# A decoder block on one core: second routing weight from its minimum, second choice, A's second values and three weight splits moved

## The chip, the cores and the metric

One Trainium2 chip, one core. The metric is the device time of one execution in microseconds; less is better. The core has TensorE (PE), VectorE (DVE), ScalarE (ACT), GpSimd (POOL) and SyncE (SP), each with its own in-order stream of instructions. Semaphores order them against each other, and they are written out by hand in this kernel.

## What is computed

`x` is 128 sequences of 64 tokens of width 128 in float32; `ctx` has the same shape.

```python
x = x + attn(layernorm(x))           # A: causal linear attention, 16 heads of 8, rope, elu + 1
x = x + xattn(layernorm(x), ctx)     # B: softmax attention over ctx, no projections, scale 8 ** -0.5
x = x + ffn(layernorm(x))            # C: shared expert + the best 2 of 8 experts

# inside ffn, xf = its input:
xn = norm(xf) * ln_scale + ln_bias
probs = softmax(xn @ gate_w.T)                     # 8 experts
tk_probs, tk_idx = top_k(probs, 2)
tk_probs = tk_probs / (sum(tk_probs) + 1e-5)
out = swiglu(xf, sWg, sWu, sWd)                    # hidden width 256
out += w[:, e] * swiglu(xf, Wg[e], Wu[e], Wd[e])   # for each e of the two chosen
```

## The kernel before

The 8192 tokens are 64 tiles of 128 and 16 groups of four tiles. The kernel has three stages.

**Steps.** A software pipeline of unrolled steps, s = -3 to 15, handles six groups at once: in step s, A's scores and values are those of group s (called a), A's projection that of f = s + 1, A's output and B's context that of h = s - 1, B's scores, softmax and values those of b = s - 2, c = s - 3 is normalised for C, and d = s - 4 is routed. Routing works on batches of two groups, so it has work only where d is odd, thus in odd steps from s = 5 on (`batch_of`, `batch_number`). Each engine has its own `step` function, and its lines are that engine's order: TensorE's at L832, ScalarE's at L1181, GpSimd's at L1494, VectorE's at L1918. In each step, scores come in four parts j = 0 to 3 (`scores`, L639), for A into `pair_x`, for B into `pair_y`; ScalarE cuts A's (`a_mask`, L1097), VectorE takes B's row maximum and subtracts it (`b_shift`, L1714 and L1718), ScalarE takes the exponential (L1126), TensorE transposes it (`b_probs_T`, L727), ScalarE copies it out (L1132), and 64 small matmuls of `a_values` (L671) or `b_values` (L744) make the values. `a_divide` (L1682, L1686) and `b_divide` (L1725 to L1733) divide by the sums on VectorE. `a_rope` (L1437) on GpSimd and `a_rotate` (L1656) on VectorE rotate queries and keys; TensorE turns and adds them (`a_q_T`, `a_k_T`, L572 and L573); `a_exp` (L1082, L1085) on ScalarE and `a_feature` (L1676) on VectorE make elu + 1. GpSimd builds the block-diagonal operands `Qblk` and `Kblk` (L1413). `c_statistics`, GpSimd's roots (L1356 to L1405), `c_norm` (L1044), `c_norm_T` (L759), its copy (L1146) and `c_logits` (L770) bring a group of C to its logits.

**Routing of a batch.** VectorE's `c_softmax` subtracts the smallest negated logit (`c_q`, zero for the best expert); ScalarE takes exp(-c_q) (`c_exp`, L1157). `c_first` marks the first choice, `c_second` finds the second minimum (L1784) and marks the second choice (L1788, L1789, `c_sel`). TensorE counts positions from `c_sel` (`c_positions`, L781 and L784), `c_index` makes indices, and `c_weights` the two weights: it multiplies both marks with the exponentials (L1800), sums the two and the whole (L1803), and divides (L1805 to L1808). It stands between the third `b_shift` and `a_divide(a, 0)`. GpSimd then scatters each token's row to its two experts' lists in DRAM (`c_scatter`, L1465), eight scatters per group, spread over the next step and a half. The last two batches are routed in the drain.

**Drain with the shared expert.** From 509 us on TensorE works the shared expert group by group (`s_up` L814, `s_down` L828, about 4.5 us per group), and the loop over 16 groups on VectorE (`drain`, L1989) and ScalarE (L1272) carries the last batches of routing and the tables between. GpSimd's drain (L1542) has the rest of the scatters and, between them, the low parts of the eight experts' weights (`split_weights`, L1482), each behind its high part from ScalarE (L1179). SyncE writes eight padding blocks once 12 groups are through `s_down` (L451, L471), then waits for all scatters (L477) and loads the first tiles (L458). TensorE transposes the first two tiles (L965) ahead of the last `s_down`.

**Routed tiles.** 135 tiles of 128 rows go through their expert (L965, L987, L997, L1009), are scaled (L1310) and scattered back by GpSimd (L1619); VectorE adds them.

Of the kernel before, what the change touches and what calls it, by code (L numbers as in the profile page):

```python
# [114 lines left out]
PAD_BEHIND = 12  # L115
E_RING = 6
TILE_BITS = 7
C_STEPS = 18
X_FIRST = 4 * GT
ROW_SLOTS = 4  # L120
B_LOADS = 4
SET_ZERO, SET_DVE = 9, 7
Y_RING = 4
# [48 lines left out]
def decoder_block(nc, x, ctx, mask, wq, wk, wv, wo, ln_scale, ln_bias, gate_w, wg, wu, wd, swg, swu, swd,  # L172
# [5 lines left out]
    with ExitStack() as stack:  # L178
# [130 lines left out]
        def tile_entry(kind, n):  # L309
# [30 lines left out]
            b_e b_eT_ps b_eTd b_av b_rc b_qt b_yd  # L340
            c_st c_ag c_xf c_cp c_var c_xfT_ps c_xfTd c_lg_ps c_lgd c_ch c_ex c_seld
# [3 lines left out]
            f_xT_ps f_xTd f_xTl w_hi w_lo f_up f_si f_hd f_hT_ps f_hTd f_dn f_yd  # L345
            y_ad y_sum y_st""".split()
# [155 lines left out]
        def _(pe):  # L502
# [329 lines left out]
            def step(s, par):  # L832
# [32 lines left out]
                scores(a, b, 2, par)  # L865
                if on(a):
                    a_values(a, 1, par)
                if on(d) and batch_of(d):
# [5 lines left out]
                if on(c):  # L874
                    c_norm_T(c, h, odd)
                if on(b):
                    b_probs_T(b, 1, a, 2)
# [92 lines left out]
            pe.wait_ge(S["ffw_in"], (2 + CH) * 16)  # L970
            pe.wait_ge(S["w_lo"], 1 + E)

# [59 lines left out]
        def _(act):  # L1032
# [111 lines left out]
            def c_norm_evac(c, par):  # L1144
                act.wait_ge(S["c_xfT_ps"], c + 1)
                act.copy(xfT[:, c * GN:(c + 1) * GN], banks[FRONT1][:, :]).then_inc(S["c_xfTd"], 1)  # L1146

            def c_second_row(c, par):

                act.wait_ge(S["c_xf"], GT * c + GT)  # L1150
                act.copy(c_row[:, c % ROW_SLOTS, :, 1, 0:D], c_row[:, c % ROW_SLOTS, :, 0, 0:D]).then_inc(S["c_cp"], 1)
# [29 lines left out]
            def step(s, par):  # L1181
# [38 lines left out]
                if on(f):  # L1220
                    a_exp(f)
                if on(b):
                    b_exp(b, 2)
# [103 lines left out]
        def _(pool):  # L1327
# [214 lines left out]
            def drain():  # L1542
# [44 lines left out]
                for n in range(GT):  # L1587
                    send(before_last, TOP * n, TOP * n + TOP)
                    if n < GT - 1:
                        split_weights(3 + n)  # L1590
                for n in range(GT):
                    send(last, TOP * n, TOP * n + TOP)
                    if n < 2:
                        split_weights(6 + n)

# [37 lines left out]
        def _(dve):  # L1633
# [139 lines left out]
            def c_first(d):  # L1773
                n, chain = c_chain(d)
                q, hit, pick = c_q[:, 0:n, :], c_hit[:, 0, 0:n, :], c_pick[:, 0, 0:n, :]
                chain(dve.scalar_tensor_tensor(hit, q, 0.0, per_expert(order, n), ALU.is_equal, ALU.mult), 4)
                chain(dve.tensor_reduce(c_m[:, 0:n], hit, AX, ALU.max), 5)
                chain(dve.tensor_tensor(pick, per_expert(order, n), per_token(c_m[:, :], n), ALU.is_equal), 6)
                chain(dve.scalar_tensor_tensor(c_t[:, 0:n, :], pick, TAKEN, q, ALU.mult, ALU.add), 7)

            def c_second(d):
                n, chain = c_chain(d)
                t, hit, pick = c_t[:, 0:n, :], c_hit[:, 0, 0:n, :], c_pick[:, 1, 0:n, :]
                chain(dve.tensor_reduce(c_min[:, 1, 0:n], t, AX, ALU.min), 8)  # L1784
                chain(dve.tensor_tensor(hit, t, per_token(c_min[:, 1, :], n), ALU.is_equal), 9)
                chain(dve.tensor_tensor(hit, hit, per_expert(order, n), ALU.mult), 10)
                chain(dve.tensor_reduce(c_m[:, 0:n], hit, AX, ALU.max), 11)
                chain(dve.tensor_tensor(pick, per_expert(order, n), per_token(c_m[:, :], n), ALU.is_equal), 12)  # L1788
                dve.tensor_tensor(c_sel[:, 0:n, :], c_pick[:, 0, 0:n, :], pick, ALU.add).then_inc(S["c_seld"], 1)  # L1789

            def slots_of(d):
                slot, n = batch_of(d)[0] % ROW_SLOTS, len(batch_of(d))
                return slice(slot, slot + n)

            def c_weights(d):

                n, chain = c_chain(d)
                dve.wait_ge(S["c_ex"], batch_number(d) + 1)
                dve.wait_ge(S["c_idxd"], batch_number(d) + 1)
                chain(dve.tensor_tensor(c_hit[:, 0:TOP, 0:n, :], c_pick[:, :, 0:n, :],  # L1800
                                        c_e[:, 0:n, :].rearrange("p (o t) e -> p o t e", o=1).to_broadcast([P, TOP, n, E]),
                                        ALU.mult), 13)
                chain(dve.tensor_reduce(c_best[:, :, 0:n], c_hit[:, :, 0:n, :], AX, ALU.add), 14)  # L1803
                m = c_m[:, 0:n]
                chain(dve.scalar_tensor_tensor(m, c_best[:, TOP, 0:n], TOP_EPS, c_best[:, 0, 0:n], ALU.mult, ALU.add), 15)  # L1805
                chain(dve.tensor_tensor(m, m, c_best[:, 1, 0:n], ALU.add), 16)
                chain(dve.reciprocal(m, m), 17)
                chain(dve.tensor_tensor(c_row[:, slots_of(d), :, :, D].rearrange("p s t n -> p n (s t)"), c_best[:, 0:TOP, 0:n],  # L1808
                                        m.rearrange("p (o t) -> p o t", o=1).to_broadcast([P, TOP, n]), ALU.mult),
                      C_STEPS)  # L1810

# [95 lines left out]
            def s_hidden(i, c):  # L1907
                dve.wait_ge(S["s_si"], i * CH + c + 1)
                dve.tensor_tensor(s_h[:, i % 2, c, :], s_sg[:, c, :], banks[S_UP[c][1]][:, :], ALU.mult)\
                    .then_inc(S["s_hd"], 1)  # L1910

            def s_add(i):
                dve.wait_ge(S["s_dn"], i + 1)
# [4 lines left out]
            def step(s, par):  # L1918
# [14 lines left out]
                if on(c):  # L1933
                    c_statistics(c)
                if on(b):
                    b_shift(b, 1)
# [26 lines left out]
            def drain():  # L1963
# [23 lines left out]
                c_first(last - 2)  # L1987
                c_second(last - 2)
                for i in range(GROUPS):  # L1989
                    s_hidden(i, 0)  # L1990
                    if i == 0:
                        b_divide(last, 1)
                    if i == 1:
                        c_weights(last - 2)
                    if i == 2:
# [3 lines left out]
                    if i == 6:  # L1999
                        c_first(last)  # L2000
                    if i == 8:
                        c_weights(last)
                    s_hidden(i, 1)
# [8 lines left out]
                    if i == 6:  # L2012
                        c_second(last)
                    if i == 7:
                        c_index(last)
# [8 lines left out]
                    if i == 12:  # L2024
                        tile_table()
                    if i:
                        s_add(i - 1)
# [10 lines left out]
            dve.wait_ge(S["set_d"], 4)  # L2038
            one_of_two = query[:, :].rearrange("p (m c) -> p c m", c=C)
# [80 lines left out]
```

## Time and profile before

| | us |
|---|---|
| median of 3 runs | 815.31 |
| lowest and highest of them | 813.89, 822.11 |
| the profiled execution's own time | 821.73 |
| its span | 819.9 |
| busy: TensorE 737.6, VectorE 596.5, ScalarE 572.3, GpSimd 553.7 | |
| mean granted clock of TensorE | 0.967 |

The span goes from the first to the last instruction of the profiled execution; times in rows count from its start. Idle time of an engine that isn't on the chain costs nothing. In a row, what stands in brackets is the idle time of the engine ahead of it and what ended it; "issue" means that the profile shows nothing that it waited for.

### The profile page before, as it was taken

What the parts mean: (1) busy time and instruction counts of PE and PEld (TensorE: products, weight loads), DVE (VectorE), ACT (ScalarE), POOL (GpSimd) and SP (SyncE); (2) the same over time, 40 slices, a digit from 0 to 9 for tenths busy, and PEclk for the clock granted to TensorE, in tenths of its full rate; (3) what the DMA queues carried; (4) which work ended last, traced back from release to release, by engine and by line L of the source; (5) the groups of instructions that cost most, each with busy time, mean ns of one, the idle gap of its engine ahead of it and who ended that gap; (6) DMA issues with size and microseconds to landing.
All of it is one profiled execution on the core that took longest, in us unless ns stands there. A gap on an engine that the chain in (4) does not pass through costs nothing.

```text
span 819.9 us, 36399 instructions
## 1 busy us (share of the span) xinstructions
PE 737.6 (90%) x14413; PEld 588.2 (72%) x14413; DVE 596.5 (73%) x1484; ACT 572.3 (70%) x1117; POOL 553.7 (68%) x706
## 2 busy tenths in 40 slices
PE   8889989988988898898898787999899999999993
PEld 4556677767766666676676565888789999987882
DVE  2335867878988987988978697669467777787773
ACT  4577879889889788988877584464256666665661
POOL 6575447469889788888877775587536666665563
PEclk9998989999999999999999898899989999999997
DMA  8421022022202203211220205010233333476673
GB/s 222 107 55 53 4 55 55 19 56 69 73 27 72 71 23 75 68 52 49 68 71 30 68 22 168 29 40 25 69 76 92 92 91 91 118 213 195 180 207 115
DMA packets 78147, 66.91 MB, mean 82 GB/s; under 512 B 8975, under 2 KB 68248, under 8 KB 77984
## 3 DMA queue, kind: packets, MB, share of 16 engines
q1 hardware_dynamic: 68512, 47.14, 22.3%
q0 software_dynamic: 8416, 16.93, 6.3%
q8 instruction: 120, 1.97, 1.0%
q10 hardware_dynamic: 1056, 0.52, 0.2%
q14 instruction: 43, 0.35, 0.2%
HBM read 42.46 MB, written 22.56 MB: 79 GB/s over the span
## 4 chain that ended last, share of the span: by engine, by line
PE 38%; issue 20%; POOL 15%; ACT 12%; DVE 10%; SPq 3%; DMA 2%; POOLq 0%; DVEq 0%; ACTq 0%
POOL mixed L1619 7%; PE pair_x L727 5%; PE pair_x L635 5%; ACT Am L1097 4%; PE bank L744 3%; POOL routed L1465 3%; PE pair_x L987 3%; PE bank L671 3%; PE bank L552 3%; ACT ExT L1132 2%; DVE mx L1714 2%; PE bank L1009 2%; DVE Ex L1718 2%; PE pair_y L627 2%; PE pair_y L635 1%
## 5 line engine op out<-in xcount | busy, mean ns | idle before, releaser
L1619 POOL DMA_INDIRECT mixed<-f_y,f_x x135 | 131.0, 971 | 91.2 <-issue 64.7
L1465 POOL DMA_INDIRECT routed<-c_row,c_idx x128 | 130.7, 1021 | 50.3 <-issue 32.9
L1305 ACT ACTIVATE qk<-pair_x 128x256 f32<-128x256 f32 x135 | 51.9, 384 | 60.8 <-PE pair_x L987 60.8
L1009 PEld LDWEIGHTS bank<-Qblk,Am 128*128 128x128 f32 x540 | 79.9, 191 | 18.9 <-issue 8.0
L1009 PE MATMUL bank<-Qblk,Am 128*128 x540 | 83.8, 278 | 2.5 <-DVE Am L2062 1.2
L1413 POOL TENSOR_TENSOR Qblk<-qT,con 128x512 f32<-128x512 f32 x64 | 66.4, 1046 | 28.4 <-DVE qT L1676 28.0
L1714 DVE TENSOR_REDUCE mx<-pair_y 128x16 f32<-128x1024 f32 x64 | 77.3, 1208 | 9.4 <-PE pair_y L635 9.4
L1097 ACT ACTIVATE Am<-pair_x 128x1024 f32<-128x1024 f32 x64 | 65.0, 1015 | 25.3 <-PE pair_x L635 25.3
L1718 DVE TENSOR_TENSOR Ex<-pair_y,mx 128x1024 f32<-128x1024 f32 x64 | 78.4, 1224 | 2.2
L1132 ACT COPY ExT<-pair_x 128x1024 f32<-128x1024 f32 x64 | 64.5, 1008 | 21.0 <-PE pair_x L727 19.4
L727 PE MATMUL pair_x<-con,Ex 128*128 128x128 f32 x512 | 68.9, 278 | 9.8 <-ACT Am L1097 9.8
L635 PE MATMUL pair_y<-Kblk,KQ 32*64 32x256 f32 x1024 | 74.3, 402 | 1.3 <-issue 1.3
L2057 DVE TENSOR_TENSOR rot<-qk,pair_x 128x256 f32<-128x256 f32 x135 | 56.8, 421 | 24.8 <-ACT qk L1305 24.5
L635 PE MATMUL pair_x<-Qblk,KQ 32*64 32x256 f32 x1024 | 73.1, 399 | 0.0
L1126 ACT ACTIVATE Ex<-Ex 128x1024 f32<-128x1024 f32 x64 | 67.3, 1052 | 3.6 <-DVE Ex L1718 3.5
L727 PEld LDWEIGHTS pair_x<-con,Ex 128*128 128x128 f32 x512 | 56.1, 141 | 16.8 <-issue 13.4
L1437 POOL TENSOR_TENSOR phi<-qk,con 128x512 f32<-128x512 f32 x32 | 35.7, 1134 | 47.6 <-ACT qk L1064 47.6
L1413 POOL TENSOR_TENSOR Kblk<-ctxT,con 128x512 f32<-128x512 f32 x64 | 66.9, 1059 | 1.0 <-PE pair_y L635 0.3
L987 PE MATMUL pair_x<-wup_hi,f_xT_hi 128*128 x135 | 65.7, 487 | 0.0
L744 PE MATMUL bank<-Cblk,ExT 128*32 128x18 f32 x4096 | 51.0, 188 | 14.5 <-issue 11.4
L744 PEld LDWEIGHTS bank<-Cblk,ExT 128*32 128x32 f32 x4096 | 43.8, 111 | 27.3 <-issue 20.5
L671 PEld LDWEIGHTS bank<-Vblk,Am 128*32 128x32 f32 x4096 | 43.4, 112 | 24.3 <-issue 21.1
(222 smaller groups left out, 1974.9 us busy)
## 6 DMA issues: line engine op xcount, KB each, us to landing
f_x<-routed SPq DMA_DIRECT2D x135, 65.0 KB, 1.9
ctxD<-in_ctx SPq DMA_DIRECT2D x32, 256.0 KB
ctxP<-in_ctx SPq DMA_DIRECT2D x16, 256.0 KB
maskB<-in_mask_BxS_if SPq DMA_DIRECT2D x16, 256.0 KB
Cblk<-mixed SPq DMA_DIRECT2D x8, 512.0 KB
Kblk<-mixed SPq DMA_DIRECT2D x8, 512.0 KB, 4.0
block_out<-X SPq DMA_DIRECT2D x14, 256.0 KB
mixed<-f_y,f_x POOLq DMA_INDIRECT x135, 2.6
```

Of the source, the lines that this page charges most:

```text
L635: return pe.matmul(banks[first_bank + q // C][half * T:(half + 1) * T, s * RH * T:(s + 1) * RH * T], stationary[rows, par, (2 * j + s) * T ...
L727: ins = pe.transpose(banks[s][:, rp * P:(rp + 1) * P], Ex[:, j % 2, rp // 2, s, rp % 2 * 2:rp % 2 * 2 + 2, :] .rearrange("p r n -> p (r n) ...
L744: ins = pe.matmul(banks[B_O][s * T + q:s * T + q + TQ, at:at + 2 * E9], ExT[:, j % 2, s, 2 * i + r, 1 - c, q:q + TQ], Cblk[:, par, 2 * j + ...
L987: ins = pe.matmul(banks[F_UP[n % 2]][:, :], x_part[:, u % 3, :], w_part[:, bass.ds(e, 1), :, :].rearrange("p o m i -> p (o m i)"), start=( ...
L1009: ins = pe.matmul(banks[F_O[n % 2]][:, 0:D], f_hT[:, u % 3, c * P:(c + 1) * P], wdn[:, bass.ds(e, 1), c, :].rearrange("p o d -> p (o d)"), ...
L1097: act.activation(Am[:, j % 2].rearrange("p i s r n -> p (i s r n)"), pair_x[:, :], ACT.Relu)\
L1132: act.copy(ExT[:, j % 2].rearrange("p s r c q -> p (s r c q)"), pair_x[:, :]).then_inc(S["b_eTd"], 1)
L1413: return pool.tensor_tensor(dst[:, j, :, :, :], both.to_broadcast([P, 2, RH, T]), rows, ALU.mult)
L1465: pool.indirect_dma_start(routed[:, :], bass.IndirectOffsetOnAxis(ap=c_idx[:, d % ROW_SLOTS, t, n:n + 1], axis=0), c_row[:, d % ROW_SLOTS, ...
L1619: pool.indirect_dma_start(mixed[:, :], bass.IndirectOffsetOnAxis(ap=f_x[:, u, D + 1:D + 2].bitcast(I32), axis=0), f_y[:, u, :], None, boun ...
L1714: dve.tensor_reduce(mx[:, j % 2, :], scores, AX, ALU.max).then_inc(S["b_mx"], 1)
L1718: dve.tensor_tensor(Ex[:, j % 2].rearrange("p i s r n -> p (i s r) n"), scores, mx[:, j % 2, :].rearrange("p (r o) -> p r o", o=1).to_broa ...
```

## The change

1. `c_weights`: the best expert's exponential is 1, and the second's is exp(-second minimum). `c_best[:, 0]` is set to 1 once; in the steps `c_best[:, 1]` comes from a new instruction on ScalarE, `c_exp_second`, which stands behind `a_exp`; VectorE sums the eight exponentials and goes on from there, with a wait for the new semaphore `c_e2` behind that sum. For the two batches of the drain VectorE makes it from the mark and the exponentials (`c_second_picked`). The chain of a batch has 17 links instead of 18.
2. `c_second` is cut: the mark of the second choice and `c_sel` become `c_chosen`, which in a step stands behind `b_divide(c, 1)` and `c_statistics(c)`. `c_first` waits for the indices of the batch before.
3. TensorE: `a_values(a, 1)` moves from ahead of `c_positions` to behind `a_k_T` and `c_norm_T`.
4. The low parts of experts 5 to 7 are made by VectorE in groups 13 to 15 of the drain. GpSimd keeps five, and sends the last group's scatters in one go. TensorE waits for both counts before the first tile.

```diff
+BY_POOL = 5
-C_STEPS = 18
+C_STEPS = 17
-SET_ZERO, SET_DVE = 9, 7
+SET_ZERO, SET_DVE = 9, 8
...
@@ TensorE, step
                 scores(a, b, 2, par)
-                if on(a):
-                    a_values(a, 1, par)
                 if on(d) and batch_of(d):
                     c_positions(d, h)
                 if on(b):
...
                 if on(c):
                     c_norm_T(c, h, odd)
+                if on(a):
+                    a_values(a, 1, par)
                 if on(b):
                     b_probs_T(b, 1, a, 2)
...
-            pe.wait_ge(S["w_lo"], 1 + E)
+            pe.wait_ge(S["w_lo"], 1 + BY_POOL)
+            pe.wait_ge(S["w_ld"], E - BY_POOL)
@@ ScalarE
+            def c_exp_second(d):
+
+                n = len(batch_of(d)) * GT
+                act.wait_ge(S["c_ch"], C_STEPS * batch_number(d) + 8)
+                act.activation(c_best[:, 1, 0:n], c_min[:, 1, 0:n], ACT.Exp, scale=-1.0).then_inc(S["c_e2"], 1)
...
                 if on(f):
                     a_exp(f)
+                if on(d) and batch_of(d):
+                    c_exp_second(d)
                 if on(b):
                     b_exp(b, 2)
@@ GpSimd, drain
-                    if n < GT - 1:
+                    if n < BY_POOL - 3:
                         split_weights(3 + n)
-                for n in range(GT):
-                    send(last, TOP * n, TOP * n + TOP)
-                    if n < 2:
-                        split_weights(6 + n)
+                send(last, 0, TOP * GT)
@@ VectorE
             def c_first(d):
                 n, chain = c_chain(d)
+                if batch_number(d):
+                    dve.wait_ge(S["c_idxd"], batch_number(d))
...
                 chain(dve.tensor_reduce(c_m[:, 0:n], hit, AX, ALU.max), 11)
+
+            def c_chosen(d):
+                n, chain = c_chain(d)
+                pick = c_pick[:, 1, 0:n, :]
                 chain(dve.tensor_tensor(pick, per_expert(order, n), per_token(c_m[:, :], n), ALU.is_equal), 12)
                 dve.tensor_tensor(c_sel[:, 0:n, :], c_pick[:, 0, 0:n, :], pick, ALU.add).then_inc(S["c_seld"], 1)
...
+            def c_second_picked(d):
+
+                n, picked = len(batch_of(d)) * GT, batch_number(d) - (BATCHES - 2) + 1
+                dve.wait_ge(S["c_ex"], batch_number(d) + 1)
+                dve.wait_ge(S["c_idxd"], batch_number(d) + 1)
+                dve.tensor_tensor(c_hit[:, 0, 0:n, :], c_pick[:, 1, 0:n, :], c_e[:, 0:n, :], ALU.mult).then_inc(S["c_pe"], 1)
+                dve.wait_ge(S["c_pe"], picked)
+                dve.tensor_reduce(c_best[:, 1, 0:n], c_hit[:, 0, 0:n, :], AX, ALU.add).then_inc(S["c_e2"], 1)
+
             def c_weights(d):
 
                 n, chain = c_chain(d)
                 dve.wait_ge(S["c_ex"], batch_number(d) + 1)
-                dve.wait_ge(S["c_idxd"], batch_number(d) + 1)
-                chain(dve.tensor_tensor(c_hit[:, 0:TOP, 0:n, :], c_pick[:, :, 0:n, :],
-                                        c_e[:, 0:n, :].rearrange("p (o t) e -> p o t e", o=1).to_broadcast([P, TOP, n, E]),
-                                        ALU.mult), 13)
-                chain(dve.tensor_reduce(c_best[:, :, 0:n], c_hit[:, :, 0:n, :], AX, ALU.add), 14)
-                m = c_m[:, 0:n]
-                chain(dve.scalar_tensor_tensor(m, c_best[:, TOP, 0:n], TOP_EPS, c_best[:, 0, 0:n], ALU.mult, ALU.add), 15)
-                chain(dve.tensor_tensor(m, m, c_best[:, 1, 0:n], ALU.add), 16)
-                chain(dve.reciprocal(m, m), 17)
+                m, e_sum, e_best = c_m[:, 0:n], c_best[:, TOP, 0:n], c_best[:, 0:TOP, 0:n]
+                chain(dve.tensor_reduce(e_sum, c_e[:, 0:n, :], AX, ALU.add), 13)
+                dve.wait_ge(S["c_e2"], batch_number(d) + 1)
+                chain(dve.tensor_scalar(m, e_sum, TOP_EPS, 1.0, ALU.mult, ALU.add), 14)
+                chain(dve.tensor_tensor(m, m, c_best[:, 1, 0:n], ALU.add), 15)
+                chain(dve.reciprocal(m, m), 16)
...
+            def split_weights(e):
+
+                dve.wait_ge(S["w_hi"], e + 2)
+                dve.tensor_tensor(wup_lo[:, e, :, :], wup[:, e], wup_hi[:, e, :, :], ALU.subtract).then_inc(S["w_ld"], 1)
...
                 if on(c):
                     c_statistics(c)
+                if on(d) and batch_of(d):
+                    c_chosen(d)
                 if on(b):
                     b_shift(b, 1)
@@ VectorE, drain: c_chosen directly behind each c_second, c_second_picked ahead of each c_weights, and
+                    if i >= GROUPS - (E - BY_POOL):
+                        split_weights(E - (GROUPS - i))
                     if i:
                         s_add(i - 1)
@@ set-up
+            dve.memset(c_best[:, 0, :], 1.0).then_inc(S["set_d"], 1)
```

## Rows read from the trace of the kernel before

**Rows 1.** The page: shares of the chain by engine; then one group, GpSimd's tile scatters

```profile
PE 38%; issue 20%; POOL 15%; ACT 12%; DVE 10%; SPq 3%; DMA 2%; POOLq 0%; DVEq 0%; ACTq 0%
...
L1619 POOL DMA_INDIRECT mixed<-f_y,f_x x135 | 131.0, 971 | 91.2 <-issue 64.7
```

**Rows 2.** Chain that ended last, around the end of the drain: start, us, what

```profile
586.45 2.42 DMA routed<-c_row,c_idx
```

**Rows 3.** GpSimd's timeline near the end of the drain: start us, us, what

```profile
570.05 1.71 POOL L1482 TENSOR_TENSOR wup_lo<-KQ,wup_hi 128x512 fp32r<-128x512 f32 x1 [0.57 <-ACT wup_hi L1179]
571.93 0.99 POOL L1465 DMA_INDIRECT routed<-c_row,c_idx  x1 [0.16 <-issue]
573.22 0.97 POOL L1465 DMA_INDIRECT routed<-c_row,c_idx  x1 [0.30 <-issue]
...
576.86 1.32 POOL L1482 TENSOR_TENSOR wup_lo<-KQ,wup_hi 128x512 fp32r<-128x512 f32 x1
```

**Rows 4.** Timelines of SyncE's queue and of TensorE, 574 to 598

```profile
576.62 8.56 SPq L451 DMA_DIRECT2D routed<-pad  x8
589.69 2.56 SPq L458 DMA_DIRECT2D f_x<-routed  x3
...
587.20 1.95 PE L828 MATMUL bank<-shared_down_w,Vblk 128*128 128x128 f32 x16
591.65 0.41 PE L965 MATMUL pair_y<-con,f_x 128*128 128x128 f32 x1 [2.51 <-DMA f_x<-routed]
...
593.00 3.62 PE L828 MATMUL bank<-shared_down_w,Vblk 128*128 128x128 f32 x16
```

**Rows 5.** Windows: stretch, length, busy us of each engine (count), PEclk, DMA share, GB/s

```profile
167.00:171.00 4.00, 3.85 (x110) 2.70 (x108) 3.03 (x11) 3.68 (x6) 2.22 (x5) 1.00 0.05 16
459.50:463.00 3.50, 2.78 (x84) 1.67 (x92) 1.31 (x4) 1.62 (x2) 3.25 (x10) 0.50 0.06 19
593.00:595.00 2.00, 2.00 (x11) 2.00 (x11) 0.29 (x1) 0.27 (x1) 0.00 (x0) 0.50 0.24 60
```

**Rows 6.** TensorE's timeline: first and last of five gaps behind A's second values

```profile
165.17 0.24 PE L744 MATMUL bank<-Cblk,ExT 128*32 128x18 f32 x2 [1.25 <-issue]
...
457.25 0.24 PE L744 MATMUL bank<-Cblk,ExT 128*32 128x18 f32 x4 [2.69 <-issue]
```

**Rows 7.** L1800 and L1157 by source (ns min/median/max); VectorE's timeline at 586

```profile
L1800 DVE TENSOR_TENSOR c_hit<-c_pick,c_hit x8: 281/1140/2691, 166.6 to 554.2; 128x128 f32<-128x128 f32 x8
...
L1157 ACT ACTIVATE c_hit<-c_q x8: 238/246/258, 148.2 to 547.3; 128x64 f32<-128x64 f32 x8
...
586.67 0.69 DVE L1909 TENSOR_TENSOR Vblk<-phi,pair_y 128x512 f32<-128x512 f32 x1 [1.32 <-ACT phi L1173]
```

**Rows 8.** Timelines of VectorE, ScalarE, TensorE, 399 to 412; ScalarE, TensorE, 170 to 177

```profile
400.09 2.56 DVE L1800 TENSOR_TENSOR c_hit<-c_pick,c_hit 128x128 f32<-128x128 f32 x1
...
403.07 0.17 DVE L1805 SCALAR_TENSOR_TENSOR c_m<-c_best 128x8 f32<-128x8 f32 x1
...
405.90 0.68 DVE L1676 SCALAR_TENSOR_TENSOR qT<-bank,qk 128x512 f32<-128x512 f32 x1
...
408.35 1.22 DVE L1718 TENSOR_TENSOR Ex<-pair_y,mx 128x1024 f32<-128x1024 f32 x1
...
405.04 1.04 ACT L1126 ACTIVATE Ex<-Ex 128x1024 f32<-128x1024 f32 x1
...
411.03 0.39 PE L627 MATMUL pair_y<-bias,couple 64*128 64x512 bf16 x2 [0.40 <-issue]
...
170.81 1.04 ACT L1126 ACTIVATE Ex<-Ex 128x1024 f32<-128x1024 f32 x1
...
176.90 0.39 PE L627 MATMUL pair_y<-bias,couple 64*128 64x512 bf16 x2 [0.40 <-issue]
```

**Rows 9.** Timelines of VectorE and TensorE, 386 to 394

```profile
386.82 1.06 DVE L1788 TENSOR_TENSOR c_pick<-con,c_m 128x64 f32<-128x64 f32 x1
...
393.90 0.39 PE L627 MATMUL pair_y<-bias,couple 64*128 64x512 bf16 x2 [0.82 <-DVE Ex L1718]
```

More of the change, by code:

```diff
@@ L340, in decoder_block @@
             b_e b_eT_ps b_eTd b_av b_rc b_qt b_yd
[L341 removed]
+            c_st c_ag c_xf c_cp c_var c_xfT_ps c_xfTd c_lg_ps c_lgd c_ch c_ex c_e2 c_pe c_seld
             c_ps c_posd c_read c_idxd c_put c_next c_tick c_sc0 c_sc1 c_sc2 c_sc3
@@ L344, in decoder_block @@
             s_xh s_xl s_up s_si s_hd s_dn s_ac
-            f_xT_ps f_xTd f_xTl w_hi w_lo f_up f_si f_hd f_hT_ps f_hTd f_dn f_yd
+            f_xT_ps f_xTd f_xTl w_hi w_lo w_ld f_up f_si f_hd f_hT_ps f_hTd f_dn f_yd
             y_ad y_sum y_st""".split()
@@ L1782, in c_second @@
                 n, chain = c_chain(d)
-                t, hit, pick = c_t[:, 0:n, :], c_hit[:, 0, 0:n, :], c_pick[:, 1, 0:n, :]
+                t, hit = c_t[:, 0:n, :], c_hit[:, 0, 0:n, :]
                 chain(dve.tensor_reduce(c_min[:, 1, 0:n], t, AX, ALU.min), 8)
@@ L1798, in c_weights @@
                 dve.wait_ge(S["c_ex"], batch_number(d) + 1)
-                dve.wait_ge(S["c_idxd"], batch_number(d) + 1)
-                chain(dve.tensor_tensor(c_hit[:, 0:TOP, 0:n, :], c_pick[:, :, 0:n, :],
-                                        c_e[:, 0:n, :].rearrange("p (o t) e -> p o t e", o=1).to_broadcast([P, TOP, n, E]),
-                                        ALU.mult), 13)
-                chain(dve.tensor_reduce(c_best[:, :, 0:n], c_hit[:, :, 0:n, :], AX, ALU.add), 14)
-                m = c_m[:, 0:n]
-                chain(dve.scalar_tensor_tensor(m, c_best[:, TOP, 0:n], TOP_EPS, c_best[:, 0, 0:n], ALU.mult, ALU.add), 15)
-                chain(dve.tensor_tensor(m, m, c_best[:, 1, 0:n], ALU.add), 16)
-                chain(dve.reciprocal(m, m), 17)
-                chain(dve.tensor_tensor(c_row[:, slots_of(d), :, :, D].rearrange("p s t n -> p n (s t)"), c_best[:, 0:TOP, 0:n],
+                m, e_sum, e_best = c_m[:, 0:n], c_best[:, TOP, 0:n], c_best[:, 0:TOP, 0:n]
[4 more added lines that the diff above has]
+                chain(dve.reciprocal(m, m), 16)
+                chain(dve.tensor_tensor(c_row[:, slots_of(d), :, :, D].rearrange("p s t n -> p n (s t)"), e_best,
                                         m.rearrange("p (o t) -> p o t", o=1).to_broadcast([P, TOP, n]), ALU.mult),
@@ L1988, in drain @@
                 c_second(last - 2)
+                c_chosen(last - 2)
                 for i in range(GROUPS):
@@ L1993, in drain @@
                     if i == 1:
+                        c_second_picked(last - 2)
                         c_weights(last - 2)
@@ L2001, in drain @@
                     if i == 8:
+                        c_second_picked(last)
                         c_weights(last)
@@ L2013, in drain @@
                         c_second(last)
+                        c_chosen(last)
                     if i == 7:
@@ L2037, in _ @@
             dve.tensor_tensor(query[:, :], ident[:, 0:T], ident[:, T:2 * T], ALU.add).then_inc(S["set_d"], 1)
-            dve.wait_ge(S["set_d"], 4)
+            dve.wait_ge(S["set_d"], 5)
             one_of_two = query[:, :].rearrange("p (m c) -> p c m", c=C)
```

## Prediction

> **What bounds the kernel now.** I read the chain of work that ended last first, then the timelines of the engines that it names, then granted clock by window. The chain has no single owner: TensorE 38%, "issue" 20%, GpSimd 15%, ScalarE 12%, VectorE 10% [rows 1]. So each edit has to be priced at its own place. There are three.
>
> The steps (about 29 us each, up to 499 us). In the middle of a step ScalarE runs without a gap and TensorE waits for it. In an odd step, where a batch of eight tiles is routed, VectorE carries more than in an even one.
>
> The drain (509 to 590 us). TensorE is full, but the chain that ends last is GpSimd's: one scatter after the other behind the last product of `c_weights` (L1808), the last one's landing from 586.45 on [rows 2], then SyncE's loads and the first tile.
>
> The routed tiles (from 590 us). GpSimd sends the 135 tiles off one after the other, 0.97 us each and half a microsecond of "issue" between (64.7 us for 126) [rows 1]: it paces the stage from the first one on. Nothing there is edited, so the stage moves as a block.
>
> **The change, part by part.** All sums are against the profiled execution: 821.73 us, span 819.90, so 1.83 lies around it. The median of the runs shown is 815.31; I take the same difference from it.
>
> *Three splits leave GpSimd.* The first one stands for 0.57 of waiting, 1.71 of work and 0.16 to the next scatter, 2.44 us, where two scatters in a row have 0.30 between them: 2.14 saved. The other two cost 1.32 and again some 0.17, 1.2 saved each [rows 3]. Together 4.5: the last scatter lands at 584.4 and not 588.9. But another chain is next. SyncE's eight padding writes start at 576.62 behind TensorE's twelfth group and are issued until 585.2 [rows 4]; of 65 KB each, like the tile loads, they should land 1.9 later, near 587.1. So the first load moves from 589.69 by about 1.8, not by 4.5. TensorE is free at 589.15 (587.20 + 1.95) and now waits 2.51 for the first tile; that shrinks to some 0.75, with a second pause of 0.8 for the second tile, whose load is issued 1.1 later (three loads in 2.56) [rows 4]. That brings a second gain. Behind the pause of now the last `s_down` took 3.62 us against 1.95, at clock 0.50 [rows 4, 5], and the first two tiles some 0.5 more. A pause of 1.25 left the clock at 1.00, one of 2.69 took it to 0.50 [rows 5, 6]. The two pauses together, 1.55, lie nearer to the first. I take 1.8 + 1.7 + 0.5 = 4.0 saved. Bounds: 1.8 (clock falls all the same) and 4.5.
>
> The trace shows a fall behind a long pause and none behind a shorter one. The Trainium skill (TensorE: Matmul & The Clock Gate, What's actually happening) says that the gate goes by how busy the array was lately, not by one pause, so two short ones with a 0.3 us transpose between them may act as one. By that rule the sum would keep 1.8 of the 4.0.
>
> VectorE takes the three splits in the last three groups. A product over the same 128x512 (L1909) takes 0.69, and VectorE waits 0.7 to 1.3 us for ScalarE ahead of each one there [rows 7]; a split delays one `s_add` whose bank is needed a group later. So: nothing. Without that cover it would be 2.1.
>
> *`c_weights`.* Before: the product L1800 (0.28 undisturbed), a sum over 192 elements, then four small ones of 0.2 to 0.25 each with their gaps (the first at 403.07) [rows 7, 8]; 1.6 in all. After, in a step: one sum over a third of the elements (some 0.2), then again four small ones. In the drain a product and a sum more stand ahead, some 0.25 each: 1.6, no change. In four of the steps L1800 takes 2.0 to 2.7 [rows 7, 8] because GpSimd builds two blocks just then. That is VectorE's time, yet it is no gain, by the next point.
>
> *The new wait.* `c_weights` now waits for an exponential on ScalarE that stands behind `a_exp`. VectorE comes to `c_weights` at 400.09; `a_exp` is over at 405.04, where L1126 follows it [rows 8]. Behind the wait on VectorE stand both divisions, `a_feature`, the fourth `b_shift`; the first scores of the next step need that. From there (call it E): the exponential 0.2 (over 8 elements; the one over 64 takes 0.25 [rows 7]); four small instructions and the two divisions 2.83 (403.07 to 405.90); feature and shift 3.67 (405.90 to the end of L1718, 409.57); start of TensorE 0.14. Sum: L627 at E + 6.84. In the five odd steps that have an `a_exp` it now stands at E + 6.09, 6.74, 5.94, 6.77, 5.99 (the first and the last shown) [rows 8]. So 0.75, 0.10, 0.90, 0.07, 0.85 later, 2.7 together. In the two small ones another path counts: A's third values wait for A's division (E + 1.9, where they start at E + 1.4 and 1.6), and ScalarE is 0.2 longer: 0.5 for both instead of 0.2. Sum 3.0 lost. Bounds: 0.2 per step for the exponential alone, 1.0; and the whole lateness of `a_feature` (E + 3.03 against 0.13, 2.33, 1.39, 1.95 and 0.86), 8.5.
>
> *Second choice behind the statistics.* In two steps the marking collides with GpSimd's rotation: L1788 and L1789 take 1.06 and 0.97 instead of 0.22, and L627 then waits 0.82 for VectorE [rows 9]. Behind the division and the statistics, 2.5 us later, the rotation is over, so two waits of 0.8 go: 1.6 gained. The positions are needed some 7 us on. That c's statistics, and GpSimd's root with them, come earlier I count at nothing: ScalarE is busy until it wants them. Bounds 0 and 3.0 (VectorE's whole loss).
>
> The row shows two VectorE instructions held by one on GpSimd. The Trainium skill (SBUF — State Buffer, Who interferes with whom) says that a VectorE instruction with two SBUF inputs contends with a GpSimd one that reads SBUF, and that `tensor_scalar` may contend too. By it, the marking would meet the small operations for c's root that the statistics have just released; at 0.2 each (six steps) the sum would lose 1.2.
>
> *A's second values behind the keys.* 64 matmuls, 0.7 us, go behind `c_norm_T`. The keys come 0.7 earlier but ScalarE is busy until the transposed tokens anyway, and `b_probs_T` starts 0.2 later inside the same cover. I take 0. Bounds: 0.2 in 16 steps, 3.2 lost; or, since two runs of 64 short matmuls no longer stand together, the five gaps of TensorE that lie there (1.25 the first, 2.69 the last, 7.8 in all) gone [rows 6].
>
> *The rest.* `c_first` waits for the indices of the batch before, which VectorE itself wrote in an earlier step: nothing. One memset more in the set-up lies beside the loads of the weights: nothing, and 0.1 without them.
>
> Net: 3.0 − 1.6 − 4.0 = −2.6 us: 819.1 for the profiled execution, 812.7 for the median.
>
> **The rivals.**
> *The gaps go.* TensorE's gaps "issue" come where short matmuls are dense: five in b's values, the keys or c's transposes right behind A's second values. Spread out, they vanish: −7.8 more, 804.9. Against it: three of the places that stay dense have gaps too, and behind a gap ScalarE is often late anyway. [...]
> *The wait for the exponential is passed on whole.* The place is VectorE at `c_weights`; it decides once the next step has no slack left for late queries and shift. Price 8.5 for 3.0: −2.6 + 5.5 = +2.9, 818.2, slower than before. For it: chain and ScalarE are tight there. Against it: VectorE idles 2 to 3 us early in the next step.
> *The clock falls again* at 591: 1.8 for 4.0, −0.4, 814.9.
> *The splits weren't the drain's bound*, because the pads land later than thought: drain 0 and the rest as forecast, +1.4, 816.7.
>
> **How the numbers follow.** Chances: forecast 0.45, gaps 0.15, exponential 0.15, clock 0.17, pads 0.08. Each but the first is one departure from the forecast; the range goes from the gaps' 805 to 820 (exponential and clock together, 820.4). A measurement tells about 1%, 8.2 us, from no change. Faster by that needs the gaps: 0.17. Slower by that needs 823.5, exponential, 3.2 for the moved values and no gain in the drain: 0.06. Within: 0.77.
>
> **What would show it.** Right: no L1482 after the fifth; last scatter near 582; first L965 near 590; `s_down` 1.95 at clock 1.00. An idle of 3 to 5 us on VectorE ahead of the second instruction of `c_weights`, released by ScalarE, five times; L627 of the next step released by VectorE's shift. L1788's line at 0.22 throughout. Wrong: last scatter early and first load not; odd steps longer by over 1 us each; TensorE's "issue" idle before 500 us well under 20 us.

## The result, and the profile after the change

The changed kernel takes 819.03 us (median of 20 runs, 816.01 to 829.01) against 814.30 (20 runs) for the kernel before: ratio 1.0051, 95% interval 1.003 to 1.0072, so 2.4 to 5.9 us slower. A second series of the same kernel, g1 below, gave 1.0072. The forecast was 2.6 us less. The profiled execution took 826.73 us, span 824.2; single executions of one kernel differ by up to 15 us, so a single profile shows where time goes better than how much.

The chain of work that ended last, by engine:

```profile
PE 38%; issue 18%; DVE 14%; ACT 12%; POOL 12%; SPq 3%; DMA 2%; POOLq 0%; DVEq 0%; ACTq 0%
```

VectorE had 10% of it and GpSimd 15% [rows 1]: the end is reached through VectorE more often. Where, its timeline in the step of [rows 8] tells:

```profile
401.26 0.21 DVE L1822 TENSOR_REDUCE c_best<-c_hit 128x8 f32<-128x64 f32 x1
406.95 0.17 DVE L1824 TENSOR_SCALAR c_m<-c_best 128x8 f32<-128x8 f32 x1 [5.48 <-ACT c_best L1154]
...
409.73 0.68 DVE L1683 SCALAR_TENSOR_TENSOR qT<-bank,qk 128x512 f32<-128x512 f32 x1
410.33 0.68 DVE L1683 SCALAR_TENSOR_TENSOR KQ<-bank,qk 128x512 f32<-128x512 f32 x1
```

ScalarE's timeline there, and TensorE's up to the next step's first scores, L628 (L627 in the kernel before):

```profile
405.69 1.06 ACT L1087 ACTIVATE qk<-qk 128x1024 f32<-128x1024 f32 x1
406.65 0.19 ACT L1154 ACTIVATE c_best<-c_min 128x8 f32<-128x8 f32 x1
406.75 1.04 ACT L1128 ACTIVATE Ex<-Ex 128x1024 f32<-128x1024 f32 x1
...
413.44 0.59 ACT L1122 COPY KQ<-bank 128x512 f32<-128x512 f32 x1 [1.72 <-PE bank L716]
```

```profile
411.06 1.06 PE L771 MATMUL bank<-gateT,xfT 128*128 128x8 f32 x8 [0.39 <-DVE KQ L1683]
412.05 0.77 PE L672 MATMUL bank<-Vblk,Am 128*32 128x18 f32 x64
412.75 0.66 PE L716 MATMUL bank<-con,b_xn 128*128 128x128 f32 x4
...
414.13 0.39 PE L628 MATMUL pair_y<-bias,couple 64*128 64x512 bf16 x2 [0.40 <-ACT KQ L1122]
```

The new wait is there: 5.48 us of idle VectorE, released by ScalarE's small exponential. Call E the start of the third exponential of B (L1126, now L1128), 406.75. `a_feature` starts at E + 2.98, as forecast (3.03). But L628 stands at E + 7.38 and not at E + 6.84. TensorE's logits (L771) wait for `a_feature`, whose bank they overwrite; behind them come 64 products of A's values, the four transposes of B's tokens, ScalarE's copy of them, and only then L628: 3.12 from the end of `a_feature` (411.01). In all five odd steps that have an `a_exp`, L771 starts 4.31 to 4.32 behind E, released by `a_feature`.

The drain, in the timelines of SyncE's queue, of GpSimd and of TensorE:

```profile
584.47 8.81 SPq L452 DMA_DIRECT2D routed<-pad  x8
596.90 9.10 SPq L459 DMA_DIRECT2D f_x<-routed  x9
```

```profile
589.89 0.97 POOL L1475 DMA_INDIRECT routed<-c_row,c_idx  x1 [0.30 <-issue]
```

```profile
595.06 1.95 PE L829 MATMUL bank<-shared_down_w,Vblk 128*128 128x128 f32 x16
598.79 0.33 PE L966 MATMUL pair_y<-con,f_x 128*128 128x128 f32 x1 [1.78 <-DMA f_x<-routed]
599.80 0.48 PE L966 MATMUL bank<-con,f_x 128*128 128x128 f32 x1 [0.68 <-DMA f_x<-routed]
600.07 3.41 PE L829 MATMUL bank<-shared_down_w,Vblk 128*128 128x128 f32 x16
```

The last scatter, seen from the steps' last L627 (499.05 before, 506.60 after), ends 4.1 us earlier (88.4, now 84.3); the first load of a tile moves by 0.3 only (90.6, now 90.3).
```profile
594.00:597.00 3.00, 3.00 (x22) 2.62 (x20) 1.80 (x3) 1.09 (x2) 0.00 (x0) 1.00 0.03 5
597.00:599.00 2.00, 0.22 (x2) 0.14 (x1) 0.77 (x2) 0.00 (x0) 0.00 (x0) 1.00 0.16 33
600.00:603.00 3.00, 3.00 (x15) 3.00 (x15) 0.29 (x1) 0.27 (x1) 0.00 (x0) 0.50 0.29 67
```

The marking of the second choice (its durations in ns: least, median, most) no longer collides, as forecast; in the kernel before it took 1.06 in [rows 9] and 1.09 at most:

```profile
L1801 DVE TENSOR_TENSOR c_pick<-con,c_m x8: 190/192/225, 155.9 to 556.4; 128x64 f32<-128x64 f32 x8
```

### The profile page after: what moved, and what is told of

It is laid out like the page before. It is cut to its first block, busy times and chain, and to the rows that moved or that the text cites. A ratio compares the mean times of both kernels' runs of the same rounds, so it can differ in the third digit from the quotient of the medians.

```text
span 824.2 us, 36412 instructions
## 1 busy us (share of the span) xinstructions
PE 736.9 (89%) x14413; PEld 584.8 (71%) x14413; DVE 582.6 (71%) x1484; ACT 571.4 (69%) x1123; POOL 549.1 (67%) x703
## 3 DMA queue, kind: packets, MB, share of 16 engines
q8 instruction: 119, 1.95, 1.1%
## 4 chain that ended last, share of the span: by engine, by line
PE 38%; issue 18%; DVE 14%; ACT 12%; POOL 12%; SPq 3%; DMA 2%; POOLq 0%; DVEq 0%; ACTq 0%
POOL mixed L1626 8%; PE pair_x L728 4%; PE pair_x L636 4%; ACT Am L1099 3%; PE bank L553 3%; PE bank L745 3%; PE pair_x L989 3%; PE bank L672 2%; DVE Ex L1725 2%; DVE mx L1721 2%; PE bank L1011 2%; PE bank L829 2%; ACT ExT L1134 2%; PE pair_y L815 2%; PE bank L771 2%
## 5 line engine op out<-in xcount | busy, mean ns | idle before, releaser
L1128 ACT ACTIVATE Ex<-Ex 128x1024 f32<-128x1024 f32 x64 | 67.3, 1051 | 3.4 <-DVE Ex L1725 3.2
L672 PE MATMUL bank<-Vblk,Am 128*32 128x18 f32 x4096 | 51.2, 188 | 17.7 <-ACT Am L1099 9.0
L1320 ACT ACTIVATE f_y<-bank,f_x 128x128 f32<-128x128 f32 x135 | 49.6, 368 | 15.6 <-PE bank L1011 8.1
```

What stands on the lines that cost most here:

```text
L672: ins = pe.matmul(num[s * T + q:s * T + q + TQ, r // RH, :, r % RH, :], Am[:, j % 2, r // RH, s, r % RH, q:q + TQ], Vblk[:, par, 2 * j + s ...
```

## The experiments

Three measures are read from every profile. *Ten periods*: from A's exponential (L1085 of the kernel before) in step 4 to the same in step 14, ten steps later. Five of them hold the place of the new wait (odd) and five hold the marking (even). *First result*: the first tile scatter (L1619 of before), counted from the steps' last L627. The ratio is to the kernel before, run on the same chip: e1 to e4 on one, f1 to f4 on a second, g1 to g4 on a third, h1 to h3 on a fourth. It rests on 6 runs of e4, f1, g3 and g4, 10 of h1, 12 of each of the others and 20 of the changed kernel; the other columns are of one profiled execution each.

| kernel | even | odd | ten periods | first result | ratio (95%) |
|---|---|---|---|---|---|
| before | 149.4 | 143.2 | 292.6 | 105.1 | |
| h2 before again | 147.1 | 143.5 | 290.7 | 103.3 | 1.0011 (0.9985-1.0037) |
| e2 splits only | 148.9 | 143.8 | 292.6 | 101.4 | 1.0019 (0.9996-1.0043) |
| e3 values only | 152.9 | 140.5 | 293.5 | 103.7 | 1.0025 (0.9991-1.0059) |
| f4 marking only | 146.5 | 143.1 | 289.6 | 103.2 | 0.9951 (0.9924-0.9978) |
| changed | 147.5 | 148.1 | 295.6 | 103.6 | 1.0051 (1.0030-1.0072) |
| g1 changed again | 147.5 | 148.9 | 296.3 | 102.6 | 1.0072 (1.0036-1.0108) |
| h1 splits back | 144.4 | 153.0 | 297.4 | 105.9 | 1.0079 (1.0046-1.0113) |
| e4 weights, splits | 147.9 | 148.9 | 296.8 | 101.2 | 1.0112 (1.0074-1.0151) |
| e1 early exponential | 144.8 | 141.8 | 286.6 | 103.1 | 0.9978 (0.9951-1.0006) |
| f2 e1, values back | 147.6 | 141.2 | 288.8 | 102.5 | 0.9936 (0.9906-0.9965) |
| f3 e1, marking back | 153.5 | 139.9 | 293.5 | 102.1 | 0.9968 (0.9934-1.0001) |
| g2 weights behind | 144.7 | 141.9 | 286.7 | 100.9 | 0.9955 (0.9929-0.9981) |
| f1 e1, early pads | 146.2 | 141.5 | 287.7 | 99.1 | 0.9880 (0.9846-0.9914) |
| h3 f1, splits back | 147.5 | 140.6 | 288.1 | 103.4 | 0.9946 (0.9915-0.9976) |
| g3 f1 with g2's move | 144.7 | 141.1 | 285.8 | 97.9 | 0.9896 (0.9862-0.9930) |
| g4 f1, values back | 143.8 | 142.7 | 286.5 | 97.9 | 0.9852 (0.9822-0.9883) |

**The wait.** Theory W: the wait for the exponential made the odd steps longer. Its rival, theory V: A's second values did.

e1 is the changed kernel with the small exponential earlier in ScalarE's `step`:

```
                     b_exp(b, 1)
+                if on(d) and batch_of(d):
+                    c_exp_second(d)
                 if on(c):
                     c_norm(c, odd)
...
                     a_exp(f)
-                if on(d) and batch_of(d):
-                    c_exp_second(d)
```

Expected of e1:

> The changed kernel with the exponential of the second weight moved up in ScalarE's order, to behind the second exponential of B, about 9 us ahead of the cut of A's exponential; all else as changed. Theory W (the wait): VectorE no longer waits some 5 us in c_weights, L628 of the next step stands 5.9 to 6.8 us behind the start of the third exponential of B instead of 7.4, the five odd steps get 5.5 us back in all, and the time is 5 us under the changed kernel, 0.998 of the kernel before (812 to 814). Theory V (A's second values behind the keys cost it): the wait goes but the time stays within 1.5 us of the changed kernel, 1.004 to 1.006 of before.

e3 moves one call in TensorE's `step` of the kernel before, as shown; e4 is the changed kernel with this call and `c_chosen(d)` back at their old places:

```
                 scores(a, b, 2, par)
-                if on(a):
-                    a_values(a, 1, par)
...
                     c_norm_T(c, h, odd)
+                if on(a):
+                    a_values(a, 1, par)
```

Expected of e3:

> The kernel before with A's second values behind the keys and c's transposes, and nothing else. Theory W: no cost of its own, 0.998 to 1.002 of before; the idle times of TensorE that nothing explains fall from 22.7 us to some 16 with no gain in time. Theory V: the cost of the change is here, 1.004 or more.

Expected of e4:

> The changed kernel with A's second values and the marking of the second choice back at their old places, so that only the new weights with their wait and the moved splits stay. Theory W: the wait costs 5.5 us in five odd steps, the splits give 1 to 2 back, the marking's collision with the rotation is back (two waits of 0.8 to 1 us): 3.5 to 5 us over before, 1.004 to 1.006. Theory V: at or under the time of before, 0.998 to 1.001.

g1 is the changed kernel unaltered; g2 moves one call on VectorE:

```
-                if on(d) and batch_of(d):
-                    c_weights(d)
                 if on(a):
                     a_divide(a, 0)
...
                     a_feature(f, odd)
+                if on(d) and batch_of(d):
+                    c_weights(d)
```

Expected of g1:

> The changed kernel, unaltered, on the same chip as the three that follow. 1.005 of before, 1.003 to 1.007, as first measured; L628 7.4 us behind the third exponential's start in five steps, ten periods 295 to 297 us.

Expected of g2:

> The changed kernel with c_weights behind a_feature on VectorE; the exponential stays where the change put it, behind a_exp. Theory F (the wait costs only because both divisions and a_feature stand behind it): a_feature starts at some 0.1 us behind the end of a_exp, L628 at 5.9 to 6.2 behind the third exponential's start, ten periods 286 to 288 us, 0.8 to 1 per cent under the changed kernel. Theory C (the odd steps are longer for ScalarE's extra instruction and TensorE's logits whatever VectorE does): L628 stays at 7 or more and the time within 2 us of the changed kernel.

The same step in e1, VectorE and TensorE (E is 394.69):

```profile
390.12 0.21 DVE L1822 TENSOR_REDUCE c_best<-c_hit 128x8 f32<-128x64 f32 x1
390.37 2.33 DVE L1824 TENSOR_SCALAR c_m<-c_best 128x8 f32<-128x8 f32 x1
...
395.32 0.68 DVE L1683 SCALAR_TENSOR_TENSOR qT<-bank,qk 128x512 f32<-128x512 f32 x1
```

```profile
400.63 0.39 PE L628 MATMUL pair_y<-bias,couple 64*128 64x512 bf16 x2 [0.40 <-ACT KQ L1122]
```

The five distances from E to the next L627 are 7.40, 7.38, 7.49, 7.38, 7.38 in the changed kernel and 7.39 to 7.76 in e4; in e1 they are 5.93, 7.07, 5.93, 6.70, 5.94, in g2 5.93 to 6.42. All four profiles with the wait ahead of the feature (the changed kernel, g1, h1, e4) have odd periods of 148 to 153 us, all others 139.9 to 143.8. V fell: e3 has no cost in the odd steps (140.5), and its 1.0025 has an interval that reaches 1.000. e4's odd periods bear W out, but its 1.0112 lies well over the expected 1.004 to 1.006. What made it 9 us slower its profile doesn't show; that execution was the fastest of e4's six, 816.87 against a median of 820.16. g2 keeps the exponential late and the wait stays harmless:

```profile
399.82 0.69 DVE L1683 SCALAR_TENSOR_TENSOR qT<-bank,qk 128x512 f32<-128x512 f32 x1
400.43 0.68 DVE L1683 SCALAR_TENSOR_TENSOR KQ<-bank,qk 128x512 f32<-128x512 f32 x1
401.03 0.21 DVE L1822 TENSOR_REDUCE c_best<-c_hit 128x8 f32<-128x64 f32 x1
401.27 0.17 DVE L1824 TENSOR_SCALAR c_m<-c_best 128x8 f32<-128x8 f32 x1
```

Theory F held: g2 is 1.2% under g1 by the ratios. So it isn't the wait that costs but what stands behind it on VectorE. That the path then runs through the logits is read from the rows; no run moved the logits.

**The marking.** f4 is the kernel before with the marking split off from `c_second` and placed as in the changed kernel; f3 is e1 with the marking back at its old place:

```
                     c_statistics(c)
+                if on(d) and batch_of(d):
+                    c_chosen(d)
```

Expected of f4:

> The kernel before with the marking of the second choice behind the division and the statistics, and nothing else. As forecast: both instructions at 0.22, two waits of 0.8 to 1.0 of L627 for VectorE gone, ten periods 290.6 to 291.2 instead of 292.6, time 0.998. If the marking and the early statistics are what the early exponential's kernel gains: 288 or less and 0.994.

Expected of f3:

> The changed kernel with the early exponential, and the marking of the second choice back right behind its comparison, ahead of the division and the statistics. If the marking collides with GpSimd's rotation as in the kernel before: L1788 and L1789 of before take about 1 us in two or more steps, the ten periods take 288 to 289 us, 1.6 to 2 more than with it moved; time 1.000. If the collision came from elsewhere: 286.6 and 0.998.

f4 lies between its two expectations: ten periods 289.6, ratio 0.9951. The forecast counted one wait of TensorE per collision. A collision in e3, on VectorE, GpSimd and TensorE, shows two:

```profile
266.69 1.06 DVE L1788 TENSOR_TENSOR c_pick<-con,c_m 128x64 f32<-128x64 f32 x1
267.79 0.96 DVE L1789 TENSOR_TENSOR c_sel<-c_pick 128x64 bf16<-128x64 f32 x1
```

```profile
266.64 2.03 POOL L1437 TENSOR_TENSOR phi<-qk,con 128x512 f32<-128x512 f32 x2 [0.82 <-ACT qk L1064]
```

```profile
273.78 0.39 PE L627 MATMUL pair_y<-bias,couple 64*128 64x512 bf16 x2 [0.82 <-DVE Ex L1718]
...
277.35 0.30 PE L572 MATMUL bank<-con,rot 128*128 128x128 f32 x1 [0.90 <-DVE c_hit L1825]
```

Against f4, VectorE stays 1.3 to 1.9 us late through the step, the keys (L572) wait too, for the bank that the positions hold, and the step up to ScalarE's next A exponential is 2.35 longer. The six profiles with the marking at its old place have even periods of 147.1 to 153.5, mean 150.0; the eleven with it moved 143.8 to 147.6, mean 145.9. f3's expectation missed in size (6 us and not 2) and in the ratio (0.9968 and not 1.000). In the two with the moved values and the old marking, e3 and f3, both instructions are slow together in four and in three steps, against two, one, two and two in the kernel before, h2, e2 and e4. So the price seems to hang on where the rotation falls against the marking; no run set that apart.

**The values.** f2 and g4 are e1 and f1 with the reverse of e3's edit.

Expected of f2:

> The changed kernel with the early exponential, and A's second values back ahead of B's first values. If the moved values are worth something once the wait is gone: the ten periods of the steps take 290 to 293 us instead of 286.6, and the time is 1.002 or more. If they are worth nothing, as forecast: 286 to 288 and the time of the early exponential, 0.998.

Expected of g4:

> The changed kernel with the early exponential and the early padding writes, and A's second values back at their old place. If the moved values are worth nothing: 0.988 like the kernel that has them moved. If the 1.6 us between ten-period sums of 287.2 and 288.8 are theirs: 0.990.

Neither expectation was met, and the two runs don't decide it. By the ten periods f2 is 1.6 us above the mean of e1 and f1 (287.2), g4 1.2 below f1; by the ratios both are the faster of their pair, by 0.4% and 0.3%, with intervals that meet and on different chips. Their worth stays open within 3 us.

**The drain.** Theory P (pads): SyncE's padding writes hold the first load of a tile once the scatters end earlier. Theory S: the scatters alone held it.

e2 is the kernel before with the change's `split_weights` on VectorE alone; g3 is f1 with g2's edit, and f1 is e1 with this:

```
-PAD_BEHIND = 12
+PAD_BEHIND = 11
```

Expected of e2:

> The kernel before with the three splits of weights moved to VectorE and nothing else. Theory P (pads: SyncE's padding writes land 3.6 us behind their last issue and hold the first load): the last scatter goes 4 us earlier, the first load of a tile only 0.5 to 0.9 us, and the time falls by 1 to 2 us, 0.998 of before. Theory S (GpSimd's scatters were the bound, as forecast): first load 1.8 us or more earlier, s_down in the pause at full clock, time 4 us lower, 0.995.

Expected of f1:

> The changed kernel with the early exponential, and SyncE's padding writes behind the eleventh group of the shared expert instead of the twelfth (PAD_BEHIND 11 for 12). Theory P (pads bind the first load): the writes go 4.5 us earlier, the first load of a tile follows the last scatter's landing and stands 86 to 87 us behind the last L627 of the steps instead of 89.5 to 90.3, TensorE no longer waits ahead of tile 0, s_down there takes 1.95 and the first scatter of a result comes at 99 to 100 instead of 101.3 to 103.7; time 2 to 3 us under the early exponential alone, 0.995 of before. Theory S (pads are not what the load waits for): load and time unchanged.

Expected of g3:

> The changed kernel with the early exponential, c_weights behind a_feature and the padding writes behind the eleventh group. If c_weights ahead of the divisions still costs something in the odd steps: one to two us under the pads-and-exponential kernel, 0.986 of before. If those steps are bound by ScalarE once the wait is gone: the same as it, 0.988.

SyncE's queue in f1, and TensorE there, with no wait and `s_down` at 1.95:

```profile
566.40 8.84 SPq L452 DMA_DIRECT2D routed<-pad  x8
579.88 5.20 SPq L459 DMA_DIRECT2D f_x<-routed  x5
```

```profile
581.96 1.95 PE L829 MATMUL bank<-shared_down_w,Vblk 128*128 128x128 f32 x16
583.74 0.27 PE L966 MATMUL pair_y<-con,f_x 128*128 128x128 f32 x1
583.85 0.27 PE L966 MATMUL bank<-con,f_x 128*128 128x128 f32 x1
583.96 1.95 PE L829 MATMUL bank<-shared_down_w,Vblk 128*128 128x128 f32 x16
```

P holds: the load at 86.3, the first result at 99.1. g3 and g4 repeat it (97.9). In time f1 gained more than expected (0.988 and not 0.995). g3's 0.9896, on another chip, is not under f1's 0.9880, so once the exponential is early, `c_weights` ahead of the divisions shows no further cost. In e2 the last scatter came 4 to 5 us earlier and the load 0.6 to 1.2, against h2 and the kernel before, as P says, but the ratio of 1.0019 shows nothing of the expected 1 to 2 us.

Three more runs were for the size of the drain's term and the rest of the loss. h1 and h3 are the changed kernel and f1 with the splits back on GpSimd, whose loop is then as before (VectorE's three calls and TensorE's second wait go with it):

```
-                    if n < BY_POOL - 3:
+                    if n < GT - 1:
                         split_weights(3 + n)
-                send(last, 0, TOP * GT)
+                for n in range(GT):
+                    send(last, TOP * n, TOP * n + TOP)
+                    if n < 2:
+                        split_weights(6 + n)
```

Expected of h1:

> The changed kernel with the three splits back on GpSimd; the rest as changed. If the moved splits give the 1.8 us that the profiles show: 1.8 above the changed kernel, 1.007 to 1.009 of before; last scatter 88 us behind the last L627 of the steps, first result's scatter at 103.7 to 105. If they give nothing or cost something in time: 1.003 to 1.006.

Expected of h2:

> The kernel before, unaltered: 1.000, 0.997 to 1.003; ten periods 292 to 293 us, first result's scatter at 103 to 105 us behind the last L627 of the steps.

Expected of h3:

> The changed kernel with the early exponential and the padding writes behind the eleventh group, and the splits back on GpSimd. Theory P (two chains of nearly equal length, pads and scatters): with the pads out of the way GpSimd's scatters bind, the first load stands at 90 as in the kernel before, and the gain of the early writes is gone: 0.993 to 0.997 of before. If the splits are worth nothing even here: load at 86 and 0.988.

h3 settles the two chains. Its GpSimd and SyncE's queue, with the last L627 of the steps at 494.14:

```profile
581.13 0.98 POOL L1473 DMA_INDIRECT routed<-c_row,c_idx  x1 [0.30 <-issue]
```

```profile
584.31 5.83 SPq L458 DMA_DIRECT2D f_x<-routed  x6
```

With the pads early and the splits on GpSimd, the load is at 90.2 again, as the last scatter demands (88.0), and 0.9946 stands against 0.9880 with the splits moved. Each edit alone is worth little, both together 4 to 6 us. With the pads where they were, the moved splits bring the first result from 104.2 (mean of five profiles: before, h2, e3, f4, h1) to 102.2 (mean of eight): 2.0, in which the load's part is 1.0. That is in the profiles; in time e2 shows no gain, and h1 is slower than the changed kernel by 1.7 us with intervals that overlap.

h1's first result, at 105.9, and its last scatter, at 89.2, came later than expected. h1 also shows a further loss. Two of its odd steps have L627 at E + 8.95 and 9.02 instead of 7.39. TensorE there, with its granted clock by window:

```profile
406.76 0.92 PE L671 MATMUL bank<-Vblk,Am 128*32 128x18 f32 x64 [1.72 <-ACT Am L1097]
407.62 1.88 PE L727 MATMUL pair_x<-con,Ex 128*128 128x128 f32 x8
```

```profile
402.00:406.00 4.00, 2.81 (x105) 1.64 (x103) 0.92 (x5) 3.97 (x7) 3.75 (x10) 1.00 0.02 6
406.00:410.00 4.00, 3.23 (x76) 3.13 (x77) 3.90 (x8) 3.22 (x7) 1.82 (x5) 0.72 0.01 4
410.00:414.00 4.00, 3.82 (x77) 2.80 (x77) 2.24 (x5) 1.47 (x3) 3.02 (x3) 0.50 0.07 21
```

Behind an idle of 1.72 us the clock went from 1.00 to 0.50, and L727 took 1.88 instead of 1.09. The idle alone doesn't decide it: TensorE's timeline of the changed kernel has the same 1.72 in this step, and there the clock stayed at 1.00 up to the next step.

```profile
408.77 0.88 PE L672 MATMUL bank<-Vblk,Am 128*32 128x18 f32 x64 [1.72 <-ACT Am L1099]
```

Each run lists its mean granted clock. Averaged over the runs of a series, it is 0.974 to 0.977 in the four with the wait (changed 0.9758, g1 0.9753, h1 0.9736, e4 0.9772; 48 runs) and 0.980 to 0.987 in every other, 0.983 in 108 runs of the kernel before. The difference of 0.008 is 0.008 x 817 / 0.5, an estimate of some 13 us more at the lower clock in each run. At half speed they cost at most half of that, and less where TensorE would have waited anyway. That the wait's longer idles bring the falls is likely and not shown.

## Why the prediction was wrong

Two terms of the sum failed, and both were off to the same side: the wait cost twice what was forecast, and the drain gave half.

*The new wait*, forecast +3.0: the right mechanism in the right place, the size too small. Odd periods: 143.5 (mean of before, h2, e2) and 150.0 (mean of changed, g1, h1), so +6.5. The step that failed is "Sum: L627 at E + 6.84": it followed the path over feature and shift and took no account of the logits, whose bank `a_feature` holds. The five distances sum to 37.0 in the changed kernel and in g1, to 32.2 on average in the kernel before, h2 and e2 (31.5, 32.4, 32.6): 4.8, which is what the odd periods of these two show (+4.9). The rest is h1's two steps at the lower clock, which the forecast of this edit did not have at all. 6.5 lies between the forecast's 3.0 and the 8.5 of the rival "passed on whole". That this rival's 818.2 came nearest to the 819.03 is luck: its wait is 2.0 too dear and its drain 2.0 too generous.

*Second choice behind the statistics*, forecast -1.6: even periods 148.5 and 146.4 (means of the same profiles), -2.0; but -1.0 in the changed kernel and g1 and -4.1 in h1. f4, with this edit alone, has -2.0 in the even periods, -2.4 over all ten, and -4.0 us in time. Right in direction; the forecast left out the second wait on TensorE, and the size is not known to better than 1 us. The Trainium skill (SBUF — State Buffer, Who interferes with whom) says that a VectorE instruction with two SBUF inputs contends with a GpSimd one that reads SBUF; the row of e3 agrees. The loss of 1.2 that the forecast weighed by that rule is not seen: both instructions of the moved marking take 0.19 to 0.24 in every step of every profile that has it.

*The drain*, forecast -4.0: about -2.0. "They should land 1.9 later" failed: the last padding write lands 3.2 behind the start of its issue and the load stands 3.6 behind that issue's end, so the pads left room for about 1.0 and not 1.8, and the pause stayed at 1.8 with one of 0.7 behind. With it the clock's gain was lost in five of the eight profiles with the moved splits and the late pads (the changed kernel, g1, e1, f2, f3; not in e2, e4, g2). The rivals of the clock and of the pads were both partly true. In the changed kernel the clock fell behind these two pauses; in e2, with 1.78 and 0.80, it did not, and the same `s_down` took 1.96:

```profile
584.86 0.33 PE L966 MATMUL pair_y<-con,f_x 128*128 128x128 f32 x1 [1.78 <-DMA f_x<-routed]
585.98 0.33 PE L966 MATMUL bank<-con,f_x 128*128 128x128 f32 x1 [0.80 <-DMA f_x<-routed]
586.15 1.96 PE L829 MATMUL bank<-shared_down_w,Vblk 128*128 128x128 f32 x16
```

The Trainium skill (TensorE: Matmul & The Clock Gate, What's actually happening) has the gate set by how busy the array was recently. The fall behind two short pauses is in keeping with that; that the pauses alone don't decide it, e2 shows.

*A's values, shorter weights*, forecast 0: not contradicted, and open within 3 us for the values. f3 and e3 have the same ten periods, 293.5, with the new weights and without. The idle of TensorE that nothing explains fell from 22.7 to 16.5 us, counted up to 512 us (9.4 in g1), while the time rose, and it is 21.4 in g4, the fastest kernel: the rival "the gaps go" priced them as if they all lay on the path.

The sum now is 6.5 - 2.0 - 2.0 = +2.5. Measured were 2.4 to 5.9, with 4.2 for the ratio itself, and 2.9 to 8.8 in g1, with 5.9. So 1.7 to 3.4 us are left and not assigned to anything. The terms come from single profiles, which differ by 2 us in the same kernel (292.6 and 290.7 for the ten periods of the kernel before and h2). The lower mean clock of the series with the wait is a candidate that no run sets apart.

## What to carry to other kernels

Before a wait is put into an in-order stream, list what stands behind it and follow every reader and every writer of the buffers that those instructions hold, not only the path that was late before: here, by the rows, a bank shared with small logits set the price. An instruction that nobody needs soon (the weights) belongs behind those that the next step needs, and its input can then come late, as in g2. Where two chains end within 2 us of each other, move both or neither: splits and padding writes together took the first result from 104 to 98 us, and g4 (802.69 us, 0.9852) is the fastest kernel of this study.

## What was not expected of the hardware

A `tensor_scalar` over eight elements per partition on VectorE (L1824) takes 0.17 us alone, and 2.33 in e1 beside two of GpSimd's block builds; f1, f2, f3 and g4 have 2.09 to 2.34 in four steps each. The reduction ahead of it takes 0.21 in all of them, but it ends before the builds start (390.33 against 390.62) and so tests nothing. GpSimd's row in e1:

```profile
390.62 2.04 POOL L1423 TENSOR_TENSOR Kblk<-ctxT,con 128x512 f32<-128x512 f32 x2
```

The tiny instruction starts 0.25 ahead of the builds by the profile and ends at 392.70, with both of them (392.66), so it pays for both neighbours whole. In the changed kernel the wait hid this: there L1824 stands behind the wait and takes 0.17.
